# One core, adaLN condition and FFN: the first slice of the condition weights is mixed by another set of matmuls

## The reference, cut to what matters

```
def cond(x, y, weight, mask, bias):              # x (2, 2048, 512), y (2, 8), weight (8, 512, 512)
    masked_w = weight * mask[None, :, :]
    w_bot = einsum('bg,got->bot', y, masked_w)   # one mixed 512x512 matrix per batch
    return einsum('bnt,bot->bno', x, w_bot) + bias

out = x + ffn(cond(x, cond_8, weight, mask, bias), w_gate, w_up, w_down)
# ffn: down(silu(gate(h)) * up(h)), all three with ternary weights and inputs rounded to 8 bits
```

## Time and profile before

| | |
|---|---|
| median of 3 runs | 440.59 us (439.86 to 440.75) |
| the profiled execution, its own time | 440.59 us |
| its span, first to last instruction | 438.8 us |
| granted TensorE clock, mean | 0.999 |
| PE MATMUL busy | 425.5 us, 97% of the span, 2318 records |
| DVE, ACT, POOL busy | 363.5, 336.8, 205.3 us |
| bytes moved by DMA | 69.79 MB |

### The profile page before, as it was taken

One profiled execution on the slowest core, in us unless ns is written; L12 is line 12 of the kernel. 1 busy time (PEld: TensorE's weight loads), 2 busy tenths in 40 slices (PEclk: granted clock), 3 DMA queues, 4 the chain that ended last, 5 costly groups with the idle time before them and its releaser, 6 DMA issues.

```text
span 438.8 us, 7668 instructions
## 1 busy us (share of the span) xinstructions
PE 425.5 (97%) x2318; PEld 257.5 (59%) x2318; DVE 363.5 (83%) x611; ACT 336.8 (77%) x474; POOL 205.3 (47%) x221
## 2 busy tenths in 40 slices
PE   4899999999999999999999999999999999999997
PEld 0234688888744455556555565655566555556555
DVE  0327768898897988899999999899999999899992
ACT  1215988778867976888888888888888888888871
POOL 0006999999149995142432423344142333414132
PEclk9999999999999999999999999999999999999999
DMA  7999999995142337254453635535263553535375
GB/s 277 404 396 408 308 335 339 313 251 144 36 98 48 61 66 187 48 145 85 134 120 73 146 70 143 97 118 120 76 157 64 135 115 100 120 87 142 80 162 154
DMA packets 104458, 69.79 MB, mean 159 GB/s; under 512 B 87280, under 2 KB 87536, under 8 KB 102896
## 3 DMA queue, kind: packets, MB, share of 16 engines
q1 hardware_dynamic: 103712, 67.13, 56.9%
q10 hardware_dynamic: 720, 2.36, 1.5%
HBM read 40.11 MB, written 8.39 MB: 111 GB/s over the span
## 4 chain that ended last, share of the span: by engine, by line
PE 59%; DMA 14%; issue 11%; DVE 9%; ACT 5%; POOL 1%; DVEq 0%; ACTq 0%; SPq 0%; POOLq 0%
PE ps L1308 15%; DMA wc<-wc 12%; PE ps L1171 11%; PE ps L1236 10%; PE ps L1126 8%; PE ps L1206 8%; PE ps L1164 4%; ACT wc L640 3%; DVE wc L954 3%; DVE wc L988 2%; DMA wc<-wcond 2%; PE ps L1139 2%; DVE p_part L1006 1%; ACT result L660 1%; PE ps L1243 1%
## 5 line engine op out<-in xcount | busy, mean ns | idle before, releaser
L1171 PE MATMUL ps<-tern_up,qT 128*128 128x512 f16 x512 | 131.1, 379 | 0.0
L1171 PEld LDWEIGHTS ps<-tern_up,qT 128*128 (+1 forms) x512 | 50.0, 98 | 54.5 <-DVE wc L988 0.4
L1006 DVE TENSOR_REDUCE p_part<-wc 128x1 f32<-128x1536 f32 x64 | 77.9, 1217 | 1.7
L988 DVE TENSOR_TENSOR wc<-ps,xT_sb 128x512 f32<-128x512 f32 x104 | 71.1, 683 | 7.3 <-issue 3.3
L640 ACT ACTIVATE wc<-wc 128x1024 f16<-128x1024 f32 x63 | 66.0, 1051 | 4.1 <-DMA wc<-wc 2.1
L623 ACT ACTIVATE wc<-wc,p_scale 128x2048 f32<-128x2048 f32 x30 | 60.1, 2002 | 4.3 <-DVE p_scale L1053 4.3
L1236 PE MATMUL ps<-wc 128*128 128x256 f16 x480 | 62.2, 273 | 0.7 <-DVE wc L954 0.7
L954 DVE TENSOR_TENSOR wc<-wc 128x1024 f16<-128x1024 f16 x60 | 56.9, 949 | 4.5 <-DMA wc<-wc 3.6
L1236 PEld LDWEIGHTS ps<-wc 128*128 128x128 f16 x480 | 46.9, 98 | 18.6 <-issue 1.2
L455 POOL TENSOR_SCALAR out_unit<-p_max,up_step,w_mean 128x1 f32<-128x1 f32 x32 | 11.3, 355 | 99.2 <-DVE p_max L1048 99.2
L618 ACT ACTIVATE xT_sb<-ps,gate_unit 128x512 f32<-128x512 f32 x78 | 49.2, 683 | 10.9 <-PE ps L1206 10.4
(11 more groups left out here) (142 smaller groups left out, 778.3 us busy)
## 6 DMA issues: line engine op xcount, KB each, us to landing
xT_sb<-xT SPq DMA_DIRECT2D x32, 256.0 KB, 6.6
x_res<-x SPq DMA_DIRECT2D x30, 256.0 KB, 2.9
out<-result SPq DMA_DIRECT2D x29, 256.0 KB, 2.4
wc<-wcond SPq DMA_DIRECT2D x12, 512.0 KB, 13.4
wc<-w_gate SPq DMA_DIRECT2D x4, 1024.0 KB, 16.0
wc<-w_up SPq DMA_DIRECT2D x4, 1024.0 KB, 8.4
wc<-w_down SPq DMA_DIRECT2D x4, 1024.0 KB, 6.1
wc<-wcond ACTq DMA_DIRECT2D x4, 512.0 KB, 7.7
```

The costliest lines, as they stand in the source:

```text
L988: nc.vector.tensor_tensor(prod[:, par, 512 * i:512 * i + 512], ps[:, UP + i % 2], source, ALU.mult).then_inc(prod_ready, 1)
L1006: nc.vector.tensor_reduce(p_part[:, par, i:i + 1], prod[:, par, 512 * lo:512 * hi], AX.X, ALU.max, apply_absolute_value=True).then_inc(par ...
L1171: ins = nc.tensor.matmul(ps[:, UP + i % 2], tile_of(s, k), tern_up[:, i, k], start=(k == 0), stop=(k == KH - 1))
```

## The change

Slice 0 alone is mixed in another way; slices 1 to 3 keep the old one. A new array `mix_pad` holds [0 | b0 | 0 | b1 | 0], 16 columns each; POOL zeroes the three blocks of zeros (three memsets of 128x16), and DVE writes the two others before `mix_w`. With the slice [b0 | 0] for the even block and [0 | b0] for the odd one, added up in PSUM, the 32 output rows of a quarter are both blocks of batch 0 and nothing else; bank `MIX` then holds batch 0 whole, in the order in which x stands. [0 | b1] and [b1 | 0] do the same for batch 1 in bank `MIX + 1`, with the two blocks swapped, as batch 1 is kept everywhere. That makes 16 matmuls where there were 8, all four of a quarter in its own column group. Batch 0 is then multiplied by its mask on DVE straight out of PSUM (`mask_first`), and batch 1 is copied by one ACT instruction without a scale. The counts of `half_merged` begin with slice 1.

```diff
+            for i in range(3):
+                nc.gpsimd.memset(mix_pad[:, 2 * T16 * i:2 * T16 * i + T16], 0.0).then_inc(mix_pad_zero, 1)
             nc.gpsimd.memset(ones[:, :], 1.0).then_inc(ones_ready, 1)
...
-            for k in range(KH):
+            act.wait_ge(mix_psum, 2)
+            nc.scalar.activation(w_bot[:, 1, 0], ps[:, MIX + 1], ACT.Copy).then_inc(half_copied, 2)
+            for k in range(1, KH):
                 act.wait_ge(mix_psum, 2 * k + 1)
...
+                for b in range(BATCH):
+                    place = mix_pad[:, T16 + 2 * T16 * b:2 * T16 + 2 * T16 * b]
+                    nc.vector.tensor_scalar(place, fold[:, :], y_sb[:, b:b + 1], None, ALU.mult).then_inc(mix_pad_ready, 1)
                 for i, b in enumerate((0, 1, 0)):
...
+            def mask_first():
+                dve.wait_ge(mix_psum, 1)
+                dve.wait_ge(s_mask[0][0], 16)
+                nc.vector.tensor_tensor(w_bot[:, 0, 0], ps[:, MIX], mask_sb[:, 0, 0], ALU.mult).then_inc(w_bot0_ready, 1)
...
             mix_weights()
-            for k in range(KH):
+            mask_first()
+            for k in range(1, KH):
                 merge_halves(k)
...
+            def mix_first():
+                for c in range(4):
+                    pe.wait_ge(s_wc[0][c], 16)
+                    for b in range(BATCH):
+                        for half in range(2):
+                            cut = T16 * ((1, 0), (2, 3))[b][half]
+                            ins = nc.tensor.matmul(ps[32 * c:32 * c + 32, MIX + b], mix_pad[:, cut:cut + 32],
+                                                   wc[:, 0, 2 * c + half], start=(half == 0), stop=(half == 1))
+                        if c == 3:
+                            ins.then_inc(mix_psum, 1)
+
             def mix_products(k):
-                if k > 0:
-                    pe.wait_ge(half_copied, 2 * k)
-                    pe.wait_ge(half_merged, 2 * k)
+                pe.wait_ge(half_copied, 2 * k)
+                if k > 1:
+                    pe.wait_ge(half_merged, 2 * k - 2)
...
+            pe.wait_ge(mix_pad_zero, 3)
+            pe.wait_ge(mix_pad_ready, 2)
+            mix_first()
+            early_products(0, range(FIRST))
             pe.wait_ge(mix_w_ready, 3)
-            mix_products(0)
-            early_products(0, range(FIRST))
```

More of the change, by code:

```diff
@@ L113, in build @@
         mix_w = sb("mix_w", [P, 3 * T16], F32)
+        mix_pad = sb("mix_pad", [P, 5 * T16], F32)
         ident = sb("ident", [P, P], BF16)
@@ L155, in build @@
         mix_w_ready = sem("mix_w_ready")
+        mix_pad_zero = sem("mix_pad_zero")
+        mix_pad_ready = sem("mix_pad_ready")
         half_ready = sem("half_ready")
@@ L391, in apply_mask @@
             def apply_mask(k):
-                pool.wait_ge(half_merged, 2 * k + 2)
+                if k == 0:
+                    pool.wait_ge(half_copied, 2)
+                else:
+                    pool.wait_ge(half_merged, 2 * k)
                 pool.wait_ge(s_mask[1][k], 16)
@@ L842, in apply_mask @@
             def apply_mask(k):
-                dve.wait_ge(half_merged, 2 * k + 1)
+                dve.wait_ge(half_merged, 2 * k - 1)
                 dve.wait_ge(s_mask[0][k], 16)
@@ L1325, in _ @@
                 if t == MIX + 1:
-                    pe.wait_ge(half_merged, 2 * KH)
+                    pe.wait_ge(half_merged, 2 * KH - 2)
                 cond_products(t, range(KH))
```

## The result

| | before | changed |
|---|---|---|
| median, runs | 440.48 us (439.86 to 440.88), 6 | 443.54 us (442.79 to 444.51), 6 |
| ratio, 95% interval | | 1.0068 [1.0057, 1.0079] |
| profiled execution, span | 440.59, 438.8 us | 443.83, 441.8 us |

The account below looks back on a forecast made before the run. PE's work from 15.60 us on was taken to set the end. The added passes' +0.04 us there would be taken up at 25.7, summing to 0.0 against 440.59: forecast 440.6 us (chance 0.82), range 439.7 to 441.6.

Parts of the forecast that it names:

- "Nothing" for what is added at the start: Kernel start: three POOL memsets (at most 0.20 us each) and two DVE instructions (0.17 us), ready at 4.9 us, cost nothing.
- What went off ACT and DVE: Slice 0: one ACT instruction of 0.63 us and two DVE merges of 0.76 removed; nothing gained.
- PE looks past at least 9: Mix on PE: PE passes over at least 9 unstarted instructions of waiting groups; with exactly 9, the total is +0.15 us.
- none is later than quarter 3's 15.5, if the groups run independently: Slice 0's mix: quarters 0 to 2 end no later than quarter 3, at about 13.2 and 14.2 for quarters 1 and 2.
- this term of the sum, +0.04: Start of the x products: four added steps replace merge and mask, so 15.64 us instead of 15.60.
- The rival of a strict order: Slice 0's mix: PE takes passes strictly in order, x products 5.36 us late, 445.8 us in total; chance 5 in 100.
- The rival of a look-ahead that is somewhat too short: Slice 0's mix: PE looks past too few waiting passes; 441.5 to 443 us; chance 7 in 100.
- Whatever moves the start of that dense run moves the end one for one: PE's busy run from 15.60 to 400 us: a shifted start shifts the end equally, unless a later wait takes it up.
- taken up at slice 2, which was predicted as 0.14: Mix of slice 2: its last quarter lands at 25.7 us, so the first 0.14 us of a delay are absorbed.
- The mask and ACT: Slice 0: DVE's mask ready at 14.73 us, at worst 15.2, hidden by batch 1's passes; ACT's copy done by 16.4.
- The cap on a gain: Slice 2: a PE that came earlier would still wait for the last quarter's landing at 25.7 us.

Follow-up runs that it names:

- e1: Kernel before with 16 small matmuls (32 instructions) added at the start of PE's program, old mix kept: 441.93 us, ratio 1.0033.
- e11: Changed kernel without batch 1's mixing matmuls (its slice 0 copied from batch 0), PE's program as long as before: 441.02 us, ratio 1.0013 to the kernel before.
- e3: Changed kernel with 112 small matmuls at PE's start, 256 instructions more in all than before (one whole fetch): 441.47 us, ratio 1.0025 to the kernel before.
- e5: Kernel before with 16 small matmuls (32 instructions) near the end of PE's program: 440.55 us, ratio 1.0004.
- e4: Changed kernel with its mixing matmuls reordered: batch 0 of quarter c, then batch 1 of quarter c-1; 442.44 us, ratio 1.0046 to the kernel before.
- l4: One more profiled execution of e8, the kernel before with only a late head: 440.49 us.
- e8: Kernel before with two DVE products put between merge and mask of slice 0, so x products start late; PE's program unchanged: 441.27 us, ratio 1.0029.
- e9: Changed kernel with both the staggered order of e4 and 112 small matmuls at PE's start: 441.53 us, ratio 1.0031 to the kernel before.
- e2: Kernel before with 128 small matmuls at PE's start, 256 instructions, one whole instruction fetch: 441.57 us, ratio 1.0032.
- e10: Kernel before with both the 16 small matmuls of e1 and the two DVE products of e8: 442.55 us, ratio 1.0076.
- l5: Another profiled execution of e8, the kernel before with only a late head: 444.88 us.
- e12: e11 with 16 small matmuls (32 instructions) more at PE's start: 443.08 us, ratio 1.0053 to the kernel before.
- l3: First of three more profiled executions of e8, the kernel before with only a late head: 442.49 us.

## Why the prediction was wrong

**"Nothing" for what is added at the start.** This is the step that failed for most of the time. The sum priced memsets, DVE's instructions, the passes and the mask, and gave the longer PE program no price. It is worth about 1.4 us put on the kernel before (e1), 2.06 put on e11, and 2.07 is what taking it away by e3 gives back; put at the end it is worth 0.04% (e5). What went off ACT and DVE and onto POOL was put at "nothing" too; the new mix goes with another step, 0.80 us at 383, in four of its seven profiled executions, and e11, with PE's program as long as before, is 0.84 us slower. The Trainium skill, page "Runtime: NRT & Kernel Launch", section "Instruction fetch mechanics", says that instructions come in 16 KiB blocks of 256 by DMA, and that the cost of crossing to the next is mostly hidden. The traces agree with the block (16,384 bytes, one for 259 PE records on average, outside the loop's later passes); whether the crossing is hidden for the engine itself was not measured, but a transpose beside a fetch took 4.78 instead of 3.1 us, and PE paid 0.96.

**"PE looks past at least 9" and "none is later than quarter 3's 15.5, if the groups run independently".** Wrong: x products at 16.69, not 15.64; this term of the sum, +0.04, measured +1.09. The 9 is rightly read from rows 5, but from a mix in which each of the groups had few passes open. One column group with four passes still to begin held back everything behind it; with three, it did not (8.94, 11.39, 13.14). A limit for each busy group fits both rows; e4, which never has four open, starts each quarter on its landing. The rival of a strict order is wrong too, since quarter 1 ran beside quarter 0's last four passes; the Trainium skill, page "TensorE: Matmul & The Clock Gate", section "The mechanism", has matmuls start strictly in program order, and the trace does not agree. The rival of a look-ahead that is somewhat too short had the mechanism of the head, and its size (1 us), and put it at 441.5 to 443; it did not have the other 2.

**"Whatever moves the start of that dense run moves the end one for one".** Wrong: of 1.09 us, 0.13 were taken up at slice 2, which was predicted as 0.14, and about 1.0 between 78 and 110 us. Had the head been the only effect, the forecast would most likely have held (l4: 440.49; e8 at the upper clock: 440.77). This does not fit e4 well, which repairs the head alone and gains 1.1 us; with the length padded the same repair gains nothing (e9 441.53, e3 441.47).

**The mask and ACT.** Right in its result, though a good 1 us later than predicted: the mask starts at 15.15 and is over at 15.84, 0.85 us before the x products, under batch 1's passes.

**The cap on a gain.** Right: e11 starts its x products 0.81 us early and is level again behind slice 2 (0.06 us early at 32 us).

**What stays open.** The 0.25 to 0.3% of e2, e3 and e9, of which the step at 383 can explain some in e3 and e9 but none in e2. How a fetch of 16 KB, or of 8 KB, slows a transpose, which wasn't measured by itself. Whose fetches q14 carries, and why the new mix shifts them by some 0.7 us against transpose 52. A PE step of 1.1 us at 150 us in e1, e10 and l5 is seen but only in part explained: in l5 it has its slow transpose; in e1 and e10 the transpose is issued some 0.75 us later, behind an issue of 1.97 and 1.99 us, and DVE's product behind it takes 1.69 and 1.68 instead of 1.40. And, since the tiles' slack changes with PE's lateness, 1.4 (e1), 2.06 (e12) and the changed kernel's 3.0 are not one number: the late head may add to what the fetches cost, as e4 (-1.1 us) suggests.

## What to carry to other kernels

When an edit adds instructions to a long program, read the instruction queues beside the DMAs that end close to a wait. Adding some tens of instructions to PE's start moved its fetches on the straight parts of the program, and here that alone was worth up to 0.6%; an edit of the other engines went with other places of the second queue's fetches. Control for it by padding to the same length (or by a whole fetch) before an edit is judged by less than 1%. And when several column groups wait for separate landings, interleave their matmuls so that none has a long row of passes open in front of another's.

## What the hardware showed that was not expected

DMA transposes of usually 3.0 to 3.1 us took 3.5 to 5.0 us in 87 of 226 cases with an instruction fetch of 8 or 16 KB in flight, and never without one (1054 cases). SP's issue of a transpose took up to 2.62 us with a PE fetch in flight and at most 1.34 without. PE's queue shows no fetch in the later passes of PE's loop (231.8 to 403.2 us before). DVE's product of 128x1024 took 0.69 or 1.77 to 1.85 us in kernels with the new mix, and POOL's instruction beside it then 1.77 or 1.78, or 1.26 or 1.27. TensorE ran passes of a new column group past three open passes of a busy group, not past four. After 2.69 us of idle PE ahead of the x products the granted clock fell in two of five executions (l3 and l5: 0.60 and 0.74 in the stretch 16 to 20 us) and stayed at 1.00 in the others (e8, l4, e10). A PE that came 1 us later into the stretch of 78 to 110 us lost its small gaps there and was level at the end of it.
